# Storing the products of a chunk in two halves and loading its key products in two halves

## The reference, cut to what matters

```python
q, k, v = (silu(causal_dwconv(x @ W.T)) ...)      # per head 64 wide, k scaled
a, beta = sigmoid(x @ Wa.T + ba), sigmoid(x @ Wb.T + bb)
def step(S, inp):
    qt, kt, vt, at, bt = inp
    err = einsum('bhij,bhj->bhi', S, kt) - vt
    S = at[..., None] * S - bt[..., None, None] * (err[..., None] * kt[:, :, None, :])
    o = einsum('bhij,bhj->bhi', S, qt)
    return (S, o)
```

## Time and profile before

| | |
|---|---|
| median of 3 runs | 6852.53 us (6846.88 to 6866.42) |
| profiled execution | 6860.17 us |
| its span | 6857.9 us |
| DVE busy in the span | 5248.9 us (77%) |
| PE busy | 5051.4 us (74%) |
| POOL busy | 3429.3 us (50%) |
| ACT busy | 3328.6 us (49%) |
| DMA moved | 695.81 MB |

### The profile page before, as it was taken

One profiled execution on the slowest core, in us unless ns is written; L12 is line 12 of the kernel. 1 busy time (PEld: TensorE's weight loads), 2 busy tenths in 40 slices (PEclk: granted clock), 3 DMA queues, 4 the chain that ended last, 5 costly groups with the idle time before them and its releaser, 6 DMA issues. The chain is left out here.

```text
span 6857.9 us, 177748 instructions
## 1 busy us (share of the span) xinstructions
PE 5051.4 (74%) x59063; PEld 3315.4 (48%) x59063; DVE 5248.9 (77%) x15738; ACT 3328.6 (49%) x7298; POOL 3429.3 (50%) x4488
## 2 busy tenths in 40 slices
PE   3677777777777777677777637888888887888888
PEld 2555555655555555555555523444444444444443
DVE  5888988889888988888988856666666666666665
ACT  5455555455555555555555524444444444444444
POOL 1777877778877777777777851111111111111110
PEclk9777777777777777777777768888888888888888
DMA  4555555555555555555555531111111111111111
GB/s 166 139 129 140 143 143 141 133 135 145 146 144 140 138 134 144 143 145 139 137 137 143 142 87 43 47 46 46 46 46 46 46 46 46 46 46 46 46 46 34
DMA packets 1195976, 695.81 MB, mean 101 GB/s; under 512 B 1054937, under 2 KB 1106809, under 8 KB 1193596
## 3 DMA queue, kind: packets, MB, share of 16 engines
q1 hardware_dynamic: 888048, 500.99, 27.4%
q10 hardware_dynamic: 307200, 185.09, 11.0%
HBM read 371.99 MB, written 313.95 MB: 100 GB/s over the span
## 5 line engine op out<-in xcount | busy, mean ns | idle before, releaser
L1914 DVE TENSOR_REDUCE nmax<-w_bank 128x1 f32<-128x512 f32 x1024 | 641.7, 683 | 398.3 <-PE w_bank L1492 393.8
L1017 DVE SCALAR_TENSOR_TENSOR p_bank<-y,conv_w,p_bank 128x128 f32<-128x128 f32 x3072 | 822.3, 350 | 134.5 <-ACT p_bank L808 97.9
L594 POOL TENSOR_TENSOR qp<-qp,pt 128x512 f32<-128x512 f32 (+7 forms) x1024 | 844.8, 825 | 80.3
L589 POOL TENSOR_TENSOR qp<-qp,ab 128x512 f32<-128x512 f32 (+7 forms) x1024 | 843.9, 824 | 70.3
L732 PE MATMUL p_bank<-xnT,weights 128*128 128x128 f32 x4096 | 710.4, 345 | 66.0 <-ACT xnT L893 55.4
L732 PEld LDWEIGHTS p_bank<-xnT,weights 128*128 128x128 f32 x4096 | 661.6, 253 | 145.2 <-issue 145.2
L1444 POOL TENSOR_TENSOR ot<-ot,ln_w 128x1024 f32<-128x1024 f32 x64 | 150.6, 2353 | 1126.0 <-ACT ot L1752 1126.0
L591 POOL TENSOR_TENSOR pt<-qp,vb 128x512 f32<-128x512 f32 (+7 forms) x1024 | 703.5, 687 | 0.1
L1451 POOL TENSOR_TENSOR x1b<-x,weights_rest 128x256 f32<-128x256 f32 x64 | 46.3, 724 | 1166.8 <-DVE bst L2010 1166.8
L1726 ACT ACTIVATE pt<-e_bank 128x1024 f32<-128x1024 f32 x512 | 514.3, 1021 | 171.2 <-PE e_bank L1522 170.3
L1492 PE MATMUL w_bank<-ks,qs 96*128 96x512 bf16 x1024 | 393.9, 451 | 159.5 <-DMA ks<-part_dram 130.0
(11 more groups left out here) (243 smaller groups left out, 10956.0 us busy)
## 6 DMA issues: line engine op xcount, KB each, us to landing
prod_dram<-prod ACTq DMA_DIRECT2D x64, 1280.0 KB, 9.7
kp<-prod_dram SPq DMA_DIRECT2D x64, 640.0 KB, 5.5
qp<-prod_dram SPq DMA_DIRECT2D x64, 640.0 KB, 7.2
a_dram<-at ACTq DMA_DIRECT2D x64, 512.0 KB
ab<-a_dram SPq DMA_DIRECT2D x64, 512.0 KB, 5.7
v_dram<-vt ACTq DMA_DIRECT2D x64, 512.0 KB
vb<-v_dram SPq DMA_DIRECT2D x64, 512.0 KB, 4.7
vt<-e_dram SPq DMA_DIRECT2D x64, 512.0 KB
```

What stands on the lines that cost most here:

```text
L589: link(nc.gpsimd.tensor_tensor(q, q, ab[:, g, r:r + 1, :].to_broadcast([128, w, DV]), ALU.mult), 1)
L594: link(nc.gpsimd.tensor_tensor(q, q, pt2[:, 0:w], ALU.add))
L1017: nc.vector.scalar_tensor_tensor(out=zz, in0=y[:, j % Y_BANKS, i, :, tap:tap + C], scalar=conv_w[:, m, tap:tap + 1], in1=zz, op0=ALU.mult, ...
L1914: nc.vector.tensor_reduce(nmax[:, n:n + 1], bank[:], AX.X, ALU.max, negate=True).then_inc(freed, 1)
```

## The change

The store of the products becomes two stores: the first is issued after the fourth of the eight copies, the second after the eighth. Both count on `p_wr`, so who waits for it now waits for 32 in place of 16 for each step. The waits that keep `prod_dram` from being overwritten too soon move ahead of the copies. The load of `kp` becomes two loads of eight tokens each, the second with a semaphore of its own, `kp_late_in`; POOL waits for that one before it scales the later tokens, and DVE's first half waits only for the first. Nothing else is changed.

```diff
-                    sp.wait_ge(*dma_of(p_wr, n, g, 1))
+                    sp.wait_ge(*dma_of(p_wr, n, g, 1, 32))
 ...
-                    sp.dma_start(kp[:], prod_dram[o].rearrange("m (h k r) c -> (m h) k r c", h=4, k=2)[:, 0]).then_inc(kp_in[o], 16)
+                    sp.dma_start(kp[:, 0:HALF], prod_dram[o].rearrange("m (h k r) c -> (m h) k r c", h=4, k=2)[:, 0, 0:HALF]).then_inc(kp_in[o], 16)
+                    sp.dma_start(kp[:, HALF:C], prod_dram[o].rearrange("m (h k r) c -> (m h) k r c", h=4, k=2)[:, 0, HALF:C]).then_inc(kp_late_in[o], 16)
 ...
-                pool.wait_ge(*dma_of(kp_in, n, g, 0))
+                pool.wait_ge(*dma_of(kp_late_in, n, g, 0))
 ...
-                act.wait_ge(*dma_of(p_wr, n, g, 0))
+                act.wait_ge(*dma_of(p_wr, n, g, 0, 32))
 ...
             def products(s, n, g):
                 if due(dma_of(x_wr, n, g, -1, 32)[1]):
-                    act.wait_ge(*dma_of(p_wr, n, g, -1))
+                    act.wait_ge(*dma_of(p_wr, n, g, -1, 32))
                     act.wait_ge(*dma_of(x_wr, n, g, -1, 32))
-                for b in range(GB):
-                    act.wait_ge(p_filled, 8 * s + b + 1)
-                    nc.scalar.activation(prod[:, b, :], d_bank[b % 2][:, 0:4 * ROW], ACT.Copy).then_inc(p_freed, 1)
-                act.wait_ge(p_freed, 8 * s + 8)
                 if due(dma_of(qp_in, n, g, -2)[1]):
                     act.wait_ge(*dma_of(qp_in, n, g, -2))
                 if due(dma_of(kp_in, n, g, -2)[1]):
                     act.wait_ge(*dma_of(kp_in, n, g, -2))
-                act.dma_start(prod_dram[g].rearrange("m p c -> p m c"), prod[:].rearrange("p b (q c) -> p (b q) c", c=ROW)).then_inc(p_wr[g], 16)
+                    act.wait_ge(*dma_of(kp_late_in, n, g, -2))
+                for half in range(2):
+                    mine = range(GB // 2 * half, GB // 2 * half + GB // 2)
+                    for b in mine:
+                        act.wait_ge(p_filled, 8 * s + b + 1)
+                        nc.scalar.activation(prod[:, b, :], d_bank[b % 2][:, 0:4 * ROW], ACT.Copy).then_inc(p_freed, 1)
+                    act.wait_ge(p_freed, 8 * s + mine.stop)
+                    act.dma_start(prod_dram[g][4 * mine.start:4 * mine.stop].rearrange("m p c -> p m c"),
+                                  prod[:, mine.start:mine.stop].rearrange("p b (q c) -> p (b q) c", c=ROW)).then_inc(p_wr[g], 16)
```

More of the change, by code:

```diff
@@ L374, in layer0_recurrence @@
         e_wr, xe_in, x_wr, xk_in = ([sem(f"{name}{g}") for g in range(GROUPS)] for name in ("e_wr", "xe_in", "x_wr", "xk_in"))
-        a_wr, beta_wr, v_wr, p_wr, qp_in, kp_in, vb_in, ab_in, nb_in, upd_wr, xd_in, dec_wr, db_in, o_wr = (
+        a_wr, beta_wr, v_wr, p_wr, qp_in, kp_in, kp_late_in, vb_in, ab_in, nb_in, upd_wr, xd_in, dec_wr, db_in, o_wr = (
             [sem(f"{name}{g}") for g in range(GROUPS)] for name in
-            ("a_wr", "beta_wr", "v_wr", "p_wr", "qp_in", "kp_in", "vb_in", "ab_in", "nb_in", "upd_wr", "xd_in",
+            ("a_wr", "beta_wr", "v_wr", "p_wr", "qp_in", "kp_in", "kp_late_in", "vb_in", "ab_in", "nb_in", "upd_wr", "xd_in",
              "dec_wr", "db_in", "o_wr"))
```

## The result

| | before | changed |
|---|---|---|
| median of 5 runs each | 6852.53 us (6846.88 to 6877.74) | 6797.25 us (6788.12 to 6803.82) |
| ratio, 95% interval | | 0.9908 (0.9890 to 0.9925) |
| profiled execution | 6860.17 us | 6803.82 us |
| its span | 6857.9 us | 6801.6 us |

The kernel became 0.9% faster: 55 us by the medians, 63 by the ratio, where 50 were forecast (6802.5 us, against 6797.25 measured). The first thing to look at is the group rows of DVE after the change, same stretch and columns as the earlier trace rows.

A forecast was written before the change was run, and what follows sets the result against it. DVE bounds the recurrence: a slot of some 60.2 us is its work plus about 6 us idle. Waits for ACT -51, first slot -2, 3 kept back: -50 from the median 6852.53, giving 6802.5 us; range 6770 to 6850.

The forecast's parts named there:

- kp is loaded for nobody's sake: DVE's L1064: kp's load is hidden, so its halves win nothing, except 2 us off an 8.0 us first-slot wait.
- The hold: ACT's gates' store is held by the product store; halving it frees ACT 2.3 us sooner (1.1 to 3.0), gaining 51 us.
- The estimate beside it: ACT's release: if a half bore the 2.0 us fixed DMA cost in full, 1.3 us sooner, gain about 41 us.
- The load vb: SP's load now meets the first half store; costs ACT's release 0 to 1.4 us, taken as 0.4.
- The price of the added issue between the copies: ACT issues one more DMA between fourth and fifth copy, mostly in idle time; costs 0 to 0.5 us, taken as 0.3.
- What is left of the waits: DVE's 51 waits for ACT at L1017, 53.6 us: each shrinks by 2.3 us or to none, five leaving 2.2 us.
- my own sign, below 8: Expected in the profile after: DVE's 53.5 us of waits for ACT's L808 fall below 8.
- Not given back: DVE's later waits (L639, L622, xk) take back nothing of size; bound: L639 and xk could take up to the whole gain.
- Rival A: The hold goes, but DVE stands longer at L639 or xk: -5 to -15, about 6843 us; chance 0.18.
- The clock of PE: A shorter gap may keep PE above the 1.2 GHz level; priced at nothing, between 10 us lost and 15 won.
- Rival B: SP's many small rows set ACT's hold, so the added issue costs 30 us: 6883 us; chance 0.12.
- Rival C: Release sooner by more, and PE also cuts the L622 and L639 waits: -75, 6778 us; chance 0.14.

The follow-up runs named there:

- the loads alone: Kernel before with kp loaded in two halves and the product store still one DMA; ratio 1.0003.
- its two neighbours of the same order: Kernel before with the two semaphores declared but unused, 0.9998 (72.0 us of waits for ACT); kernel before with only kp's load halved, 1.0003 (87.2 us).
- gates early: Kernel before, one product store, with the gates' and betas' stores issued right behind the betas; ratio 0.9907.
- numbers 5: Kernel before, one product store, with the gates' and betas' stores issued directly ahead of the product copies; ratio 1.0069.
- 11: Kernel before, one product store, with the gates' and betas' stores at the end of ACT's slot, behind masked_scores; ratio 1.0084.
- number 10: Changed kernel with the gates' and betas' stores issued right behind the betas; ratio 0.9900.
- the stores alone: Kernel before with the product store in two halves and kp loaded by one DMA; ratio 0.9901.

## Why the prediction was right, step by step

*kp is loaded for nobody's sake.* Right: the loads alone gave 1.0003. The one wait for kp of the earlier trace rows was misread: it stands in the last slot, at 3976.7 us, and not in the first. It fell by 1.1 us (8.0 to 6.9), where I had 2.

*The hold.* The mechanism was right. I had the second half hold the gates' issue until 3.15 us behind the second store, and 0.4 more for vb; the median is 3.84 us, from 6.21. So halving the bytes took off 2.4 us and not half of 6.2; 1.5 us did not shrink. Whether that is a fixed part or what was left of the first half, no run tells. By the start of L851, ACT was free 1.9 us sooner (14.34 to 12.41), where I had 2.3; at the end of the gates' issue it was 2.2 us sooner (7.33 + 6.21 against 7.45 + 3.84). The estimate beside it, by the 2.0 us of the Trainium skill ("DMA: Bandwidth & Descriptors", Anatomy of one DMA), had 1.3 us, and the measured release lies between the two; but the skill gives this figure for DMAs that GpSimd issues, and these are issued from ACT. The load vb, which now meets the first half, lands in 6.3 us where it took 4.7 (medians), as feared, but nobody on DVE's path waits for that. The price of the added issue between the copies was small, as assumed: the last store came 0.12 us later.

*What is left of the waits.* The step that was mis-sized is "2.2 us are left". With 1.93 in place of 2.3 the same list of waits would leave 4.2 us, and 15 to 23 were measured; my own sign, below 8, was not met. I took the waits of one execution as fixed. They depend on when DVE comes, and it may come to them sooner once time is won elsewhere; this is argued, not shown. The same fault lay in the starting point: 53.5 us was a low reading of a kernel that showed 72.0 and 87.2 in its two neighbours of the same order. The lists of those two would leave 6.5 and 11.1 us. That the difference, 53 us, came close to the 51 forecast is in part luck: start and remainder were both too low, and by about as much. Even with L851 4.2 us sooner (gates early) some 23 us stay; what they wait for then I did not pursue.

*Not given back.* Right in the sum: L639, L622 and xk together rose by 9.5 us in the first profile of the changed kernel and fell by 10.3 in the second (144.8, 49.6 and 31.8 us). Rival A wanted them to take nearly all.

*The clock of PE* was priced at nothing. The 3.75 us of the projection did not change, and the mean granted clock from 300 to 3950 us was 0.755 before and 0.753 and 0.762 in the two profiles after.

*Rival B* (SP's traffic sets the hold) is out: the gates' issue fell to 2.1 us (median), and moving it away gave the gain. *Rival C* did not come. The rival that I did not name is the one of numbers 5 and 11: other orders of the same stores collide with the copies or with kp.

No version beats the changed kernel beyond the intervals; number 10 is at 0.9900, the stores alone at 0.9901.

## What to carry to other kernels

A DMA issued from a compute engine can stop that engine when a large store stands ahead of it in the same queue (here 1280 KB in 4096 rows; bytes and rows were not told apart); it shows as a long issue row and as idle time "for issue" of the next compute. Look at who waits for that engine, and take the issue away (issue it when the queue is empty) or start the large store earlier in parts; parts issued together did nothing here. And before moving a transfer, look at what starts close behind its new place: here a load 2.7 us behind it became the new limit.

## What the runs showed of the hardware that was not expected

Of three stores issued in a row from ACT (512, 512 and 8 KB) the third was held for 2.56 us, though the product store of the slot before was long done. What held it was not looked into. Half a product store lands in 6.5 us (median; 6.2 for the first halves, 7.7 for the second), the whole in 9.7, and a quarter in 5.9. With other traffic beside them, the other parts included, time falls much less than bytes.
